# Message passing on a graph: each gather waits for the engine completion of the gather before it

## What is computed

```python
Q, K, V = x @ WQ, x @ WK, x @ WV                 # each (N, 8, 16)
Eh = (edge_attr @ WE).reshape(-1, 8, 16)
score = K[src] * Q[dst] / sqrt(16) * Eh
score = exp(clip(score.sum(-1), -5, 5))
wV = segment_sum(V[src] * score, dst)
Z  = segment_sum(score, dst)
h  = x + wV / (Z + 1e-6)
y  = batchnorm(h) * gamma + beta                 # over the nodes
out = layernorm(x + y)                           # over the features
```

## Time and profile before

| | |
|---|---|
| Median of the 3 runs shown | 2724.64 us (2724.4 to 2725.85) |
| The profiled execution's own time | 2723.19 us |
| Its span | 2721.4 us, 1.8 us less than its time |
| Busy in the span | PE 79%, PEld 72%, DVE 61%, POOL 59%, ACT 27% |
| Mean granted TensorE clock | 0.617 of full speed |
| DMA | 399.30 MB, mean 147 GB/s |

### The profile page before, as it was taken

How to read it: one execution, slowest core, us unless ns; L and a number is a source line. 1 busy time by engine, 2 the same in 40 slices (tenths; PEclk the granted TensorE clock), 3 DMA queues, 4 the chain that set the end, 5 groups by cost and what they waited for, 6 DMA issues and landing times.

```text
span 2721.4 us, 50085 instructions
## 1 busy us (share of the span) xinstructions
PE 2155.3 (79%) x14458; PEld 1968.4 (72%) x14458; DVE 1652.8 (61%) x3708; ACT 740.4 (27%) x1863; POOL 1617.5 (59%) x1695
## 2 busy tenths in 40 slices
PE   7258887788888888788788888878878878887887
PEld 7147777777777777777677777767767777776777
DVE  5046666666666666666666666666666666666685
ACT  3012222222222222222222222222222222222235
POOL 0756666666666666666666666666666666666604
PEclk9555655666655666556655566566665666557578
DMA  8544544544444444454444444444444444444443
GB/s 331 149 123 140 147 144 138 146 147 144 141 143 148 137 146 145 141 148 143 142 145 143 148 138 143 148 138 150 144 140 145 144 146 139 146 147 139 143 144 95
DMA packets 220935, 399.30 MB, mean 147 GB/s; under 512 B 94554, under 2 KB 102058, under 8 KB 220124
## 3 DMA queue, kind: packets, MB, share of 16 engines
q0 software_dynamic: 79728, 217.82, 25.8%
q1 hardware_dynamic: 141044, 180.01, 22.3%
HBM read 368.11 MB, written 29.55 MB: 146 GB/s over the span
## 4 chain that ended last, share of the span: by engine, by line
DVE 36%; PE 21%; another core or an unknown queue 21%; issue 16%; DVEq 4%; ACT 2%; DMA 1%; SPq 0%; POOL 0%; ACTq 0%; POOLq 0%
DVE kq L965 8%; DVE ssum L968 8%; DVE ring L830 6%; PE eh_ps L679 6%; DVE kq L959 5%; PE agg_ps L690 4%; DVE onehot L904 3%; DVEq L908 2%; PE ohT_ps L660 2%; PE aux_ps L701 2%; PE aux_ps L700 2%; DVE acc L918 1%; PE qe_ps L670 1%; ACT ohT L509 1%
## 5 line engine op out<-in xcount | busy, mean ns | idle before, releaser
L438 POOL DMA_INDIRECT ring<-kv_rows,src_t x1661 | 1584.8, 954 | 1005.5 <-remote 553.0
L690 PE MATMUL agg_ps<-onehot,ring 128*128 128x42 f32 x3328 | 688.0, 370 | 304.0 <-issue 203.2
L690 PEld LDWEIGHTS agg_ps<-onehot,ring 128*128 128x128 f32 x3328 | 650.5, 285 | 377.8 <-issue 366.3
L679 PE MATMUL eh_ps<-we_sb,ea 128*128 128x128 f32 x3328 | 793.7, 412 | 41.8 <-issue 41.6
L959 DVE TENSOR_TENSOR kq<-ring,qe_ps 128x512 f32<-128x512 f32 x416 | 285.7, 687 | 847.1 <-remote 780.6
L679 PEld LDWEIGHTS eh_ps<-we_sb,ea 128*128 128x128 f32 x3328 | 713.0, 312 | 50.4 <-issue 50.1
L509 ACT COPY ohT<-ohT_ps 126x512 bf16<-126x512 bf16 x416 | 243.7, 586 | 850.8 <-remote 847.6
L660 PE MATMUL ohT_ps<-ident_b,onehot_b 128*126 128x128 bf16 x1664 | 257.0, 303 | 117.9 <-issue 94.5
L965 DVE TENSOR_TENSOR kq<-kq,eh_ps 128x512 f32<-128x512 f32 x416 | 286.2, 688 | 93.3 <-remote 26.5
L514 ACT ACTIVATE qe_ps<-sclip 128x32 f32<-128x32 f32 x416 | 83.6, 201 | 875.6 <-DVE sclip L970 509.1
L660 PEld LDWEIGHTS ohT_ps<-ident_b,onehot_b 128*126 128x126 bf16 x1664 | 190.5, 199 | 177.9 <-issue 152.8
(11 more groups left out here) (112 smaller groups left out, 979.8 us busy)
## 6 DMA issues: line engine op xcount, KB each, us to landing
ea<-in_edgeT SPq DMA_DIRECT2D x416, 256.0 KB
ring<-kv_rows,src_t POOLq DMA_INDIRECT x1661
q_win<-q_rows SPq DMA_DIRECT2D x416, 31.5 KB
kv_rows<-ring SPq DMA_DIRECT2D x24, 512.0 KB, 10.3
q_rows<-q_st SPq DMA_DIRECT2D x27, 360.0 KB
ring<-in_xT SPq DMA_DIRECT2D x12, 512.0 KB, 5.6
xq<-in_xT SPq DMA_DIRECT2D x25, 240.0 KB
xs<-in_xT SPq DMA_DIRECT2D x25, 240.0 KB
```

What stands on the lines that cost most here:

```text
L438: pool.indirect_dma_start(out=kv[:, s, j, :], out_offset=None, in_=kv_rows, in_offset=bass.IndirectOffsetOnAxis(ap=src_t[:, n * TILES + j: ...
L679: last = pe.matmul(eh_ps[s % 2][:, j * P:(j + 1) * P], ea[:, s % EARS, j * P:(j + 1) * P], we_sb[:, :], start=True, stop=True)
L690: pe.matmul(msg_ps[s % 2], kv[:, s, j, D:KV], onehot[:, s % 8, j, :], start=(j == 0), stop=(j == TILES - 1))
```

## The change

Every gather but the first waits until a semaphore of its own, `gather_written`, has reached the number of gathers before it. GpSimd adds 1 to this semaphore when it finishes the gather instruction. The order of the gathers, their number, their waits for `agg_ready`, and the programs of all other engines stay as they are.

```diff
@@ -185,6 +185,7 @@
         ea_landed = [sem(f"ea_landed{s}") for s in range(EARS)]
         win_landed = [sem(f"win_landed{s}") for s in range(EARS)]
+        gather_written = sem("gather_written")
         kv_landed = [sem(f"kv_landed{s}") for s in range(SLOTS)]
@@ -435,9 +436,12 @@
                 if n >= SLOTS:
                     pool.wait_ge(agg_ready, n - SLOTS + 1)
                 for j in range(TILES if n < NG - 1 else LAST_TILES):
+                    if n + j > 0:
+                        pool.wait_ge(gather_written, n * TILES + j)
                     pool.indirect_dma_start(
                         out=kv[:, s, j, :], out_offset=None, in_=kv_rows,
                         in_offset=bass.IndirectOffsetOnAxis(ap=src_t[:, n * TILES + j:n * TILES + j + 1], axis=0),
+                        engine_sem=gather_written,
                     ).then_inc(kv_landed[s], 16)
```

## The result

The changed kernel takes 2734.15 us (median of 8 runs, 2732.78 to 2735.78), the kernel before 2725.68 us in the same comparison (8 runs, 2723.07 to 2728.7). The ratio is 1.0031, interval 1.002 to 1.0042: slower by 8.5 us, a little more than the 0.2% that can be told from no change. The profiled execution of the changed kernel took 2732.89 us, 9.7 us more than the profiled one of before. Its mean granted clock is 0.630.

A forecast was written before the change was run, and what follows sets the result against it. Bound: TensorE's semaphores held back by gathers, four holds of 1.47 us plus 0.18 us per group, 400 groups. Forecast: 2723.2 us plus 8 us for the second condition, 2731 us; its own range 2722 to 2750, overall 2480 to 2960.

The forecast's parts named there:

- The forecast's case: Gather loop: distance between gather starts up to 1.4 us, the hold unbroken, 2722 to 2750 us; chance 0.36.
- the release: Rival: gathers spaced beyond the hold let TensorE's semaphores out after each one, 2474 to 2718 us; chance 0.35.
- T = 1.25 us: Distance between starts of two gathers stays 1.25 us; the wait hides in the 0.30 us between gathers.
- the hold: Time each gather on GpSimd blocks TensorE's semaphores, 1.34 to 1.47 us, four per group.
- the case of GpSimd as the bound: Rival: gather starts 1.58 to 1.71 us apart make GpSimd set the time, 2773 to 2989 us; chance 0.19.
- Nothing is released: TensorE's semaphores still come out together once a group, after the fourth gather; copy every 6.07 to 6.12 us.
- the totals of the remote waits: Sign: waits of ACT's copy, DVE's first product and POOL's gather stay at 848, 781 and 553 us.
- point of decision: Distance between gather starts above which the release brings gain: about 1.40 us, and below 1.55 us.
- rivals of the fourth gather: TensorE's semaphores come a fixed time after a group's last gather; longer distances paid three times, 2891 us; chance 0.10.
- the queued gather: Possibility within the release: the gather queued behind makes the hold, not the gather itself; below 2474 us, no separate chance.
- The 8 us of the second condition: Second wait at each group's first gather, between TensorE's semaphore and gather: 0.02 us in 400 groups, 8 us.
- the waits in the middle of a group: Added waits before a group's later gathers: cost nothing more at 1.25 us between gather starts.

The follow-up runs named there:

- second job: Repeat of the changed kernel, 2734.47 us against 2726.06 for the kernel before, ratio 1.0031; a single traced run of the kernel before took 2725.31 us.
- the increment alone: Kernel before plus each gather adding 1 to gather_written, no gather waiting: 2233.08 us (ratio 1.0002) without the hold, 2690.15 us (ratio 1.0005) with it.
- the strip of 320: Kernel before plus GpSimd clearing a 128x320 scratch tile behind each gather: 2646.1 us (ratio 1.1844) without the hold, median 2651.54 us (ratio 0.9859) with it.
- the strip of 128: Kernel before plus GpSimd clearing a 128x128 scratch tile behind each gather: 2375.82 us (ratio 1.0646) without the hold, 2695.13 us (ratio 1.002) with it.
- first job: Batch of follow-up kernels run beside the kernel before at 2232.19 us, without the hold; the increment alone took 2233.08 us in it.

## Why the prediction was right, and where it was not

The forecast's case came true, and its time is 3 us off. The prediction had given that case a chance of 0.36, and 0.35 to the release, so that it came true is weak support by itself; the mechanism has to be read from the runs.

**T = 1.25 us: right.** Of the values by which the earlier trace rows and the hold bounded it, the lowest held. The semaphore's own records put the increment 10 ns behind the end of the gather's record, the 0.30 us that follow it take the wait in, and the median distance in a group is 1.254 us, as before. With this the case of GpSimd as the bound fell.

The rule of the Trainium skill that spoke against the change (GPSIMD Engine Reference, Instruction dispatch), that a completion holds back only what waits on it, brought no cost here outside the 28 long distances: completion comes so soon that waiting on it puts nothing in series. Nor does the trace show a core that finishes markedly behind its record, the point drawn from the Trainium skill, Perfetto Trace Analysis, DMA Instruction, SWDGE (GPSIMD): the increment is 10 ns behind it.

**Nothing is released: right, outside the long distances.** L513, L963 and the next gather still come together about once in a group, and the median distance of the copies is 6.09 us. One sign failed: the totals of the remote waits did not stay at 848, 781 and 553 us, they fell to 757, 728 and 475, in part by the extra releases in the long distances.

**The size of the hold, 1.34 to 1.47 us: borne out, not measured closer.** At T = 1.336 us there is no gain, at 1.500 us the long waits are gone and GpSimd follows its own pace, as the rival of release put it. Its point of decision, about 1.40 us, was not tried with the hold present; it lies somewhere between the two. The rivals of the fourth gather and of the queued gather fell. What the change lacked for the gain is the distance: it left T alone.

**The 8 us of the second condition: right in size by chance, wrong in cause.** The step was 400 times 0.02 us between the release and the group's first gather. From the start of the copy to the start of that gather it is 1004.76 - 1004.59 = 0.17 us in the changed kernel, 1006.18 - 1006.00 = 0.18 us before; the semaphore's records put the gather 258 ns behind `agg_ready` in both. The term is 0, and the trace shows why: the second condition does have an instruction of its own, as the prediction feared, but it runs before the release and not behind it. The wait for `gather_written` in front of a group's first gather (its duration min, median and max in ns, first and last start):

```profile
L440 POOLq EVENT_SEMAPHORE  x400: 17/17/6963, 150.1 to 2601.7; - x134
```

The last starts at 2601.7, the gather behind it at 2603.0; the gather itself carries the wait for `agg_ready`. What the prediction had taken to cost nothing, the waits in the middle of a group, carries all of the change's cost: 28 long distances of 0.85 us, 23.9 us in sum, of which the hold gives more than half back. Over 14 groups, one pattern of 56 gathers, the changed kernel takes 85.74 us on average and the kernel before 85.37: 28 x 0.37 = 10.4 us, against 9.7 us between the two profiled executions. In the second job it is 85.71 and 85.39, some 9 us, against 7.8 us. The loop thus accounts for all of the difference.

That much comes back because of what the earlier trace rows had shown: a group is four holds and a release. The long distance is longer than a hold, so what TensorE has pending gets out in it, and the next release comes earlier. From first gather to first gather the group with the long distance takes 6.32 us on average, the next one only 5.75, the one behind that 6.48, the others 6.09 to 6.13; before, all 14 take 6.08 to 6.11 us. In a job without the hold the waits in the middle of a group cost 24.3 us, 1.1% in place of 0.3%.

Three ends of the prediction's ranges are a few us off its own sums (2743 for 2750, 2474 for 2480, 2955 for 2960); nothing hangs on it.

What stands at every 56th gather is **not settled**. It needs the wait (the increment alone has none of it), it comes at the same gathers in all three profiles that have it, and GpSimd idles 1.16 us with nothing to wait for: where the increment of the gather before is recorded, it comes 10 ns behind the record there too. The experiments were led by the theory of a border in GpSimd's instruction stream, which its sequencer passes unseen only when it may run ahead of the engine. The record speaks against it. Without the wait in front of a group's first gather the program is some 400 instructions shorter, and the long distances did not move. And the trace's records of instruction transfers have one within 3.5 us of 11 of the 28 late gathers, which is chance: it holds for 35% of all gathers. What repeats is a count of gathers, 56 of them or 7,168 rows, whatever stands between. A limit that counts gathers, or what GpSimd writes for their rows, would behave so; gathers of fewer rows would tell, and none were run.

## What to carry to other kernels

A wait on an engine's own completion is free only while something between its instructions covers it, as the 0.30 us do here, and it can still cost time at places that a timeline of one group doesn't show (one gather in 56): list the distances over the whole run before calling such a wait free. Where semaphores of one engine come out together and late, measure how long each instruction of the other engine holds them and compare that with the distance: here spacing of 1.34 us bought nothing, and spacing of 1.50 us made GpSimd the pace. Take the time of the kernel before in the same job as every experiment; here it moved by 22% with no change of the program.

## What was not expected of the hardware

- **The hold comes and goes.** The same program ran at 2726, at 2690 and at 2232 us. With the hold gone, the remote waits are gone and GpSimd paces the kernel at 1.255 us a gather. What switches it is open: the same chip gave 2232 and 2726 us minutes apart, and the kernel before kept its level throughout each job. The mean granted clock does not tell the two apart: it is 0.65 for the strip of 320 without the hold and 0.65 for the strip of 128 with it. A spacing of gathers that gains 1.4% where the hold is present costs 18% where it is absent, so no version that was run beats the kernel before in all surroundings.
- **SyncE's sequencer shows it too, in a few places.** One bookkeeping instruction of SyncE for each group's window of Q, its duration min, median and max in ns, in the kernel before with a hold (second job) and then in the increment alone without (first job):

```profile
L353 SPq SEQ_ASSERT  x416: 3/16/1406, 74.3 to 2618.0; - x139
```

```profile
L354 SPq SEQ_ASSERT  x416: 18/18/18, 74.2 to 2120.8; - x139
```

  It takes 18 ns each time without a hold; with it 5 take over 500 ns and the longest 1406, while the median stays at 16. In the same two traces 83 of SyncE's 901 `MOVE` instructions take over 500 ns with the hold, and none over 42 without; its `TENSOR_LOAD` reaches 1370 ns without the hold as well. On ScalarE and VectorE no `EVENT_SEMAPHORE`, `ALU_OP` or `FUSED_REGOPS` takes over 210 ns with the hold.
- **Completion of a gather instruction is prompt.** 9 to 11 ns lie between the end of its record and the semaphore, in the 1,054 of 1,661 increments that the changed kernel's trace holds. This is the end of the instruction on GpSimd, not the landing of the rows.
- **The 56th gather.** With the wait one gather in 56 starts 0.85 us late, at the same gathers in each of the three traces that have it.
